# Prologue of an adaLN, gated scan and FP4 FFN block: modulation rows of both batches from one product, reordered setup

## The reference

```python
mod = (silu(c) @ wmod).reshape(2, 6, 1, 512)       # c: (2, 512), wmod: (512, 3072)
sa, ca, ga, sb, cb, gb = (mod[:, n] for n in range(6))
ga, gb = (sign(g) * max(abs(g), 0.25) for g in (ga, gb))
h = layernorm(x) * (1 + ca) + sa                    # x: (2, 4096, 512)
xn = h / max(norm(h), eps) * 512**0.5 * gamma
q, kv, a = split(xn @ W_qkva.T, 3)                  # W_qkva: (1536, 512)
y[t] = sigmoid(a[t]) * y[t-1] + kv[t]               # scan along the tokens
x = x + ga * (q * y)
h = layernorm(x) * (1 + cb) + sb
x = x + gb * ffn(h)     # silu(gate) * up, then down; every operand quantised in blocks of 16
```

## Time and profile before

| | us |
|---|---|
| runs | 1975.07, 1972.27, 1974.67 (median 1974.67) |
| the profiled execution | 1973.16 |
| its span | 1971.4 |
| TensorE busy | 1939.8 (98%) |
| VectorE busy | 1708.0 (87%) |
| GpSimd busy | 1200.2 (61%) |
| ScalarE busy | 631.6 (32%) |

### The profile page before, as it was taken

One profiled execution on the slowest core, in us unless ns is written; L12 is line 12 of the kernel. 1 busy time (PEld: TensorE's weight loads), 2 busy tenths in 40 slices (PEclk: granted clock), 3 DMA queues, 4 the chain that ended last, 5 costly groups with the idle time before them and its releaser, 6 DMA issues.

```text
span 1971.4 us, 27185 instructions
## 1 busy us (share of the span) xinstructions
PE 1939.8 (98%) x9403; PEld 928.5 (47%) x9403; DVE 1708.0 (87%) x2106; ACT 631.6 (32%) x885; POOL 1200.2 (61%) x1072
## 2 busy tenths in 40 slices
PE   8999999999999999999999999999999999999998
PEld 3444444444444444444444444444444444444443
DVE  7777687778778999999999999999999999999985
ACT  4333433343323333232323323323323232332321
POOL 1545556465635777677667767767766766776731
PEclk9999999999999999999999999999999999999999
DMA  8865665657552433433333343343343334334232
GB/s 291 278 164 161 161 168 151 171 154 179 130 125 74 91 90 72 93 87 72 86 93 72 79 98 75 75 96 83 72 90 89 72 83 96 72 78 100 69 73 65
DMA packets 421251, 218.22 MB, mean 111 GB/s; under 512 B 359858, under 2 KB 359870, under 8 KB 421188
## 3 DMA queue, kind: packets, MB, share of 16 engines
q1 hardware_dynamic: 421188, 217.39, 44.3%
HBM read 95.43 MB, written 33.57 MB: 65 GB/s over the span
## 4 chain that ended last, share of the span: by engine, by line
PE 82%; POOL 6%; DVE 6%; issue 2%; ACT 2%; DMA 2%; SPq 1%; DVEq 0%; ACTq 0%; POOLq 0%
PE bank L1050 43%; PE bank L969 15%; PE bank L1070 14%; PE bank L1074 7%; POOL arena L556 2%; POOL arena L558 2%; DMA arena<-arena 1%; SPq L396 1%; DVE arena L1145 1%; PE bank L994 1%; DVE bn L1134 1%; PE bank L908 1%; DVE arena L1274 1%; ACT arena L708 0%; ACT arena L725 0%
## 5 line engine op out<-in xcount | busy, mean ns | idle before, releaser
L1050 PE MATMUL bank<-wgu_hi,arena 128*128 128x512 f16 (+1 forms) x3072 | 869.3, 361 | 2.0 <-DVE arena L1383 2.0
L1050 PE MATMUL bank<-wgu_lo,arena 128*128 128x512 f16 (+1 forms) x1536 | 555.0, 361 | 0.0
L969 PE MATMUL bank<-arena,wq_hi 128*128 128x512 f16 x1536 | 458.8, 380 | 8.1 <-DMA arena<-arena 8.1
L1050 PEld LDWEIGHTS bank<-wgu_hi,arena 128*128 128x128 f16 x3072 | 300.6, 98 | 310.0 <-issue 2.4
L969 PE MATMUL bank<-arena,wq_lo 128*128 128x512 f16 x768 | 292.0, 380 | 0.0
L1070 PE MATMUL bank<-wd_hi,arena 128*128 128x512 f16 x693 | 262.7, 379 | 0.1
L1070 PE MATMUL bank<-wd_lo,arena 128*128 128x512 f16 x693 | 262.6, 379 | 0.0
L969 PEld LDWEIGHTS bank<-arena,wq_hi 128*128 128x128 f16 x1536 | 149.8, 98 | 185.7 <-DMA arena<-arena 11.5
L1050 PEld LDWEIGHTS bank<-wgu_lo,arena 128*128 128x128 f16 x1536 | 150.3, 98 | 153.7
L1383 DVE SCALAR_TENSOR_TENSOR arena<-bank,small,arena 128x512 f32<-128x512 f32 (+1 forms) x192 | 134.0, 700 | 87.4 <-PE bank L1050 81.5
L648 POOL TENSOR_TENSOR arena<-arena 128x512 f32<-128x512 f32 x63 | 153.1, 2431 | 92.5 <-DVE arena L1458 92.5
(11 more groups left out here) (162 smaller groups left out, 2778.1 us busy)
## 6 DMA issues: line engine op xcount, KB each, us to landing
arena<-in_L_attn_x_dram SPq DMA_DIRECT2D x32, 1024.0 KB, 5.6
arena<-x_scratch SPq DMA_DIRECT2D x128, 256.0 KB, 3.2
x_scratch<-arena SPq DMA_DIRECT2D x16, 1024.0 KB, 4.3
out_dram<-arena SPq DMA_DIRECT2D x64, 256.0 KB, 3.1
arena<-in_L_wmod_dram SPq DMA_DIRECT2D x6, 1024.0 KB, 14.4
arena<-arena SPq DMA_TRANSPOSE x258, 3.5
wgu_hi<-in_L_ffn_w_gate_dram SPq DMA_DIRECT2D x1, 2816.0 KB, 12.4
wgu_lo<-in_L_ffn_w_up_dram SPq DMA_DIRECT2D x1, 2816.0 KB, 19.0
```

What stands on the lines that cost most here:

```text
L969: last = pe.matmul(dst[m % 2][:, :].rearrange("p (j t) -> p j t", j=NJ), w[:, k, at], uT[p][:, half, :, k, :], start=(n == 0), stop=(n == ...
L1050: last = pe.matmul(dst[n][:, 0:w], xT[p][:, half, k, :], wt[:, k, cut], start=(m == 0), stop=(m == 3 * KD - 1))
```

## The change

- `silu_wide` holds for each k 64 columns of batch 0 and 64 of batch 1: one product gives the row of batch 0 on partitions 0 to 63 and that of batch 1 on 64 to 127. Two products (ca, sa) take the place of four, and each row is copied in two halves of 64 partitions, to both halves of its target. ScalarE copies 1 + ca of both batches (four copies ahead of `apply(0, 0)`) and sa of batch 1 (two), VectorE sa of batch 0 (two).
- Twelve transposes of the identity into a bank not yet used stand on TensorE ahead of the first mix product.
- wmod part 0 comes in two DMAs, and `mix_row(1)` waits for each half.
- Scale-and-shift of group 0: GpSimd makes tiles 0 and 1, VectorE tiles 2 and 3.
- `ffn_row(0)` stands between weight tiles 3 and 4, `ffn_row(1)` behind the maxima; ScalarE copies both (`copy_early_row`). `ffn_row(2)` stays in group 0. VectorE loses `copy_row(0)` and `copy_row(1)`.
- ga's product moves behind product_a(0, 0, 0), weight tile 8 behind it, and `turn_ga` behind product_kv(0, 0, 0).
- SyncE: wmod parts 4 and 3 are loaded between the parts of W_qkva, x of group 1 only after the transposes of group 0.

```diff
@@ banks and rows
-        MIX_ROWS = ((1, 0, one_ca, 1.0, bank[0]), (0, 0, sa, 0.0, bank[1]), (1, 1, one_ca, 1.0, bank[3]),
-                    (0, 1, sa, 0.0, bank[2]))
+        WQ_BANKS = [bank[n] for n in (5, 6, 7, 4, 1, 5, 6, 7, 1, 0, 5, 6)]
+        WQ_AFTER = (0, 0, 0, 0, 0, 1, 2, 3, 5, 0, 6, 7)
+        MIX_ROWS = ((1, bank[2]), (0, bank[3]))
+        EARLY_ROWS = 2
+        EARLY_BANK = (bank[0], bank[2])
@@ sync
-                load_modulation(0)
+                for k in range(0, KD, 2):
+                    sp.dma_start(wmod_part(0)[:, k:k + 2], w_mod_part[0][:, k:k + 2]).then_inc(part0_loaded[k // 2], 16)
...
+                load_qkva(2)
+                load_modulation(ROWS[0][0])
+                load_qkva(1)
+                load_qkva(0)
+                load_modulation(ROWS[1][0])
                 load_modulation(2)
-                sp.dma_start(xs[1], x_group[1]).then_inc(xs_loaded[1], 16)
...
+                sp.dma_start(xs[1], x_group[1]).then_inc(xs_loaded[1], 16)
                 load_maximum(raw_gate, w_gate, 0)
-                for part in (4, 3, 5):
-                    load_modulation(part)
+                load_modulation(ROWS[2][0])
@@ gpsimd, adaln
-                    for j in range(NJ if i else 0):
+                    if i == 0:
+                        pool.wait_ge(mix_row_copied, 4)
+                        pool.wait_ge(sa0_copied, 2)
+                    for j in range(NJ if i else POOL_J):
@@ scalar
-                copy_mix_row(0)
+                copy_mix_row(0, 0)
+                copy_mix_row(0, 1)
                 apply(0, 0)
-                copy_mix_row(1)
+                copy_mix_row(1, 1)
                 squares(0, 0)
-                copy_mix_row(2)
+                copy_early_row(0)
                 u_hi(0, 0)
-                copy_mix_row(3)
...
-                    if n == KD:
+                    if n == KD - 1:
+                        copy_early_row(1)
+                    if n == 2 * KD:
                         copy_ga_row()
@@ tensor
+                for n in range(12):
+                    pe.transpose(bank[7][:, 0:P], ident[:, :], ident[:, :]).then_inc(warm, 1)
                 pe.wait_ge(silu_wide_ready, 1)
                 pe.wait_ge(gamma_copied, 1)
                 mix_row(0)
                 mix_row(1)
                 for n in range(4):
                     turn_wq(n)
-                pe.wait_ge(mix_row_copied, 2)
-                for n in range(4, 6):
-                    turn_wq(n)
-                mix_row(2)
-                mix_row(3)
-                pe.wait_ge(mix_row_copied, 3)
+                ffn_row(0)
+                turn_wq(4)
+                pe.wait_ge(mix_row_copied, 6)
+                pe.wait_ge(sa0_copied, 2)
                 turn_maximum(bank[3], col("part_max", 4), max_ready, max_turned)
                 spread_maximum(bank[3], col("top_diagonal", 4)[0:4, :], max_diagonal, max_all)
-                pe.wait_ge(wmod_loaded[2], 16)
-                pe.wait_ge(mix_row_copied, 4)
...
-                for n in range(6, 9):
+                ffn_row(1)
+                for n in range(5, 8):
                     turn_wq(n)
@@ tensor, group 0
                         product_a(0, 0, 0)
-                        for n in range(9, NWQ):
+                        ga_product()
+                        for n in range(8, NWQ):
                             turn_wq(n)
-                        turn_ga()
+                        pe.wait_ge(ga_row_copied, 1)
                         pe.wait_ge(wq_split, 2 * KD)
                         product_kv(0, 0, 0)
+                        turn_ga()
...
-                        for n in range(NROW):
+                        for n in range(EARLY_ROWS, NROW):
                             ffn_row(n)
@@ vector
+                dve.wait_ge(mix_row_ready, 2)
+                for half in range(2):
+                    dve.tensor_copy(sa[half * HP:(half + 1) * HP, 0, :], bank[3][0:HP, :]).then_inc(sa0_copied, 1)
                 part_maximum(0, 2)
-                dve.wait_ge(mix_row_copied, 2)
-                for j in range(NJ):
+                dve.wait_ge(mix_row_copied, 4)
+                dve.wait_ge(sa0_copied, 2)
+                for n, j in enumerate(range(POOL_J, NJ)):
...
@@ vector, group 0
                         mix(0, 0, 0, 1, True)
-                        copy_row(0)
-                        copy_row(1)
                         u_lo(1, 1)
                         copy_row(2)
```

More of the change, by code:

```diff
@@ L199, in adaln_block_kernel @@
         wmax_turned, wmax_diagonal = sem("wmax_turned"), sem("wmax_diagonal")
-        wmod_loaded = [sem(f"wmod_loaded{n}") for n in range(6)]
+        wmod_loaded, part0_loaded = [sem(f"wmod_loaded{n}") for n in range(6)], [sem(f"part0_loaded{n}") for n in range(2)]
         ident_zero, ident_ready = sem("ident_zero"), sem("ident_ready")
@@ L894, in mix_row @@
                 def mix_row(n):
-                    part, b, _, _, space = MIX_ROWS[n]
-                    pe.wait_ge(wmod_loaded[part], 16)
+                    part, space = MIX_ROWS[n]
+                    if part:
+                        pe.wait_ge(wmod_loaded[part], 16)
                     for k in range(KD):
-                        last = pe.matmul(space[:, :], silu_wide[:, b, k, :], wmod_part(part)[:, k, :],
+                        if part == 0 and k % 2 == 0:
+                            pe.wait_ge(part0_loaded[k // 2], 16)
+                        last = pe.matmul(space[:, :], silu_wide[:, k].rearrange("p b m -> p (b m)"), wmod_part(part)[:, k, :],
                                          start=(k == 0), stop=(k == KD - 1))
@@ L903, in ffn_row @@
                 def ffn_row(n):
+                    space, ready = (EARLY_BANK[n], early_row_ready) if n < EARLY_ROWS else (t_bank[0], mod_ready)
                     pe.wait_ge(wmod_loaded[ROWS[n][0]], 16)
-                    wait(pe, mod_copied, n - 1)
                     for k in range(KD):
-                        last = pe.matmul(ROW_BANK[n][0:B, :], silu_c[:, k, :], wmod_part(ROWS[n][0])[:, k, :],
+                        last = pe.matmul(space[0:B, :], silu_c[:, k, :], wmod_part(ROWS[n][0])[:, k, :],
                                          start=(k == 0), stop=(k == KD - 1))
-                    last.then_inc(mod_ready, 1)
+                    last.then_inc(ready, 1)
                 def turn_wq(n):
@@ L937, in _, with ga_product @@
                     turn_wq(n)
-                pe.wait_ge(mix_row_copied, 2)
-                for n in range(4, 6):
-                    turn_wq(n)
-                mix_row(2)
-                mix_row(3)
-                pe.wait_ge(mix_row_copied, 3)
+                ffn_row(0)
+                turn_wq(4)
+                pe.wait_ge(mix_row_copied, 6)
+                pe.wait_ge(sa0_copied, 2)
                 turn_maximum(bank[3], col("part_max", 4), max_ready, max_turned)
                 spread_maximum(bank[3], col("top_diagonal", 4)[0:4, :], max_diagonal, max_all)
-                pe.wait_ge(wmod_loaded[2], 16)
-                pe.wait_ge(mix_row_copied, 4)
-                for k in range(KD):
-                    last = pe.matmul(bank[2][0:B, :], silu_c[:, k, :], wmod_part(2)[:, k, :],
-                                     start=(k == 0), stop=(k == KD - 1))
-                last.then_inc(ga_row_ready, 1)
-                for n in range(6, 9):
-                    turn_wq(n)
+                ffn_row(1)
+                for n in range(5, 8):
+                    turn_wq(n)
+                def ga_product():
+                    pe.wait_ge(wmod_loaded[2], 16)
+                    pe.wait_ge(early_row_copied, EARLY_ROWS)
+                    for k in range(KD):
+                        last = pe.matmul(bank[2][0:B, :], silu_c[:, k, :], wmod_part(2)[:, k, :],
+                                         start=(k == 0), stop=(k == KD - 1))
+                    last.then_inc(ga_row_ready, 1)
                 def turn_ga():
@@ L1182, in part_maximum @@
                                       apply_absolute_value=True).then_inc(max_ready, 1)
+                dve.wait_ge(mix_row_ready, 2)
+                for half in range(2):
+                    dve.tensor_copy(sa[half * HP:(half + 1) * HP, 0, :], bank[3][0:HP, :]).then_inc(sa0_copied, 1)
                 part_maximum(0, 2)
[L1185 to L1186 removed]
+                dve.wait_ge(mix_row_copied, 4)
+                dve.wait_ge(sa0_copied, 2)
+                for n, j in enumerate(range(POOL_J, NJ)):
                     dve.wait_ge(xhat_ready, j + 1)
                     dve.tensor_tensor(u[:, j, :], u[:, j, :], one_ca[:, 0, :], ALU.mult).then_inc(ca0_ready, 1)
[L1189 removed]
+                    dve.wait_ge(ca0_ready, n + 1)
                     dve.tensor_tensor(u[:, j, :], u[:, j, :], sa[:, 0, :], ALU.add).then_inc(h0_ready, 1)
```

59 lines of the change are left out of this document (36 added, 23 removed).

## The result

| | before | after |
|---|---|---|
| median of 11 runs (us) | 1974.19 (1972.27 to 1976.54) | 1979.81 (1976.85 to 1983.14) |
| ratio, 95% interval | | 1.0027 [1.0019, 1.0035] |
| the profiled execution, its span | 1973.16, 1971.4 | 1983.14, 1980.2 |

5.6 us slower; 1979.3 was forecast. The profiled execution of after is the slowest of its eleven, 10.0 us above that of before; its rows show the mechanism, and the medians show its size. I read the rows in the order of the prediction.

The account below looks back on a forecast made before the run. The prediction took the adaLN chain through VectorE, not TensorE, to bound the kernel. A ga copy 5.8 us late less 0.25 of slack gave +5.55 us on a mean of 1973.8: 1979.3, range 1974.0 to 1983.5.

Parts of the forecast that it names:

- the sum: Whole kernel: D of 5.8 less 0.25 of slack makes group 4 and the kernel 5.55 us later.
- What bounds the kernel: From the prologue to group 4: the adaLN chain through VectorE decides, not TensorE's products; slack at most 0.3 us.
- The ga copy: VectorE, group 0: the turn of ga ends at S + 10.8 = 47.7, so the copy comes 5.8 us later than 41.87.
- S: Start of product_a(0) on TensorE, group 0: 36.9 instead of 35.94, bounds 35.0 and 39.
- case (a): Rival, prologue: transposes don't raise the clock; second product ends at 16.6, S = 38.9, D = 7.8, +7.5: 1981.3; chance 0.25.
- the lift: Prologue, TensorE: twelve transposes bring full clock to the first mix products, gain between 0 and 2.6 us; second ends at 14.4.
- The new wait: TensorE before group 1's first product: about 6 us waiting for mix(0,2), which VectorE ends at 83.2.
- D: Delay of the ga copy on VectorE, +5.8 us, said to reach the start of group 4 whole.
- TensorE cannot win it back: Behind group 4: the +5.55 us stays, as TensorE's later waits follow the same chain.

Follow-up runs that it names:

- experiment 1: Changed kernel with VectorE taking the statistics of group 1 between weight splits 7 and 8, ahead of the ga copy: 1972.7 us, ratio 0.9993.
- experiment 2: Kernel before with only turn_ga moved, from before product_kv(0,0,0) to behind product_a(0,0,1): 1979.63 us, ratio 1.0028.
- experiment 4: Changed kernel with 28 small matmuls behind weight tile 4, in TensorE's idle time before the maxima: 1977.36 us, ratio 1.0013.
- experiment 3: Changed kernel, two runs: without the twelve transposes 1979.35 us, ratio 1.0026; with ten matmuls in their place 1980.97 us, ratio 1.003.
- experiment 5: Changed kernel with 26 small matmuls ahead of group 1's first product, in TensorE's wait for mix(0,2): 1975.5 us, ratio 1.0006.
- experiments 7 and 8: Changed kernel with experiment 4's matmuls and group 1's statistics earlier; 7 also reorders group 1's load, scaling, squares: 1970.88 us; 8 has no such reordering: 1970.4 us.

## Why the prediction was right

The mechanism held, and so did the sum, but only because terms were off in opposite directions.

- **What bounds the kernel.** Shown by experiments 1 and 2: moving only ga's turn costs 4.9 us, freeing only the statistics takes off 7.1. The rival that TensorE's own later order costs the time falls with experiment 1, which leaves that order as it is.
- **The ga copy.** The copy was forecast at S + 10.8; it comes at S + 11.25 (49.74 - 38.49), as the turn only starts 10.8 us behind S, where the sum had it end. The copy came 7.87 us later, by case (a) 7.8; in experiment 1, where full rate followed the transposes, it came at 47.55 (forecast 47.7).
- **The start of group 0, S.** 36.9 with the lift, 38.9 without. Measured 36.30 (experiment 1) and 38.49. The reason given was partly wrong. I had u_lo(0) and the transposes 1.05 later and deciding; in experiment 1 the first u_lo stands at 27.55, not late at all (27.57 in the earlier trace rows). In the profiled execution after it is 2.1 later, but what ended last was the second FFN row at half clock: I took half of its records to be slow, as in the earlier trace rows; after idle stretches of 6.0 to 7.7 us it takes 5.33 to 6.20. The chain of u was close behind: with the row at 3.60 (experiment 4) the transposes let product_a(0) start at 38.06, so the slow row decided by 0.4 us only.
- **The lift by the transposes.** My forecast took it, the profiled execution did not have it, and in the median neither leaving the transposes out nor matmuls in their place can be told from the changed kernel (experiment 3). The profiled execution is case (a), which had a chance of 0.25; what the median execution does is not known. The Trainium skill (TensorE: Matmul & The Clock Gate, Part 4: PE-mode transpose) has it that transposes don't count as busy for the full clock; the profiled execution after agrees (six of the records behind them took 5.24 us), the one of experiment 1 does not (eight took 3.67 behind them, after 1.06 us of idle time).
- **The new wait.** Forecast about 6 us, ended at 83 (by the same sum 85 in case (a)); measured 5.81, ended at 85.15.
- **The term that was missing.** I let group 4 be late by D less 0.25: 5.55, or 7.55 without the lift. It was 8.42: the means of group 2 come 7.45 late, those of group 3 8.5 (125.86, against 117.39 before). Between them lies group 1 at half clock, the price of the wait itself. Experiment 5 takes this away: the means of group 3 are then 7.0 late, group 4 comes 1.6 us earlier, and the median falls by 4.3. In experiment 2, whose wait there is 2.76, group 1's records have the length of full clock. The Trainium skill (TensorE: Matmul & The Clock Gate, HAM oscillation) warns of this: waits for data make TensorE start the next work at half clock. The runs agree for this wait, with the numbers above.
- **"TensorE cannot win it back".** This step does not hold as it stands. Against the profile of before, the delay shrinks from 8.42 at group 4 to 7.55 at the first FFN product after the change, and from 7.93 to 3.75 in the kernel without the transposes, whose profiled execution (1979.63) is nearer to the median of after (1979.81). In the median of experiment 2, too, 6.1 us at group 4 cost 4.9.
- **Why the sum came out.** The median, 5.6 over before, lies between the forecast's 5.1 over this median and case (a) with 7.1. Three things were off: the sum counted on the lift, which the profiled execution lacked (D 7.87 instead of 5.8); it had nothing for group 1 at half clock (up to 4.3 in the median); and it let none of the delay be absorbed behind group 4. That these cancelled was luck; that the sign and the place were right was not. The profiled pair, 10.0 us apart, does not give the 5.6 us of the medians, and no trace of an execution of after near its median was taken.

## What to carry to other kernels

Before moving an instruction, look at what stands behind its consumer in another engine's stream: here a copy of 0.15 us was the gate of the next group's statistics, and moving the statistics ahead of it took off 7.1 us, where the 7 us of mix products removed in front of a wait went into the wait (1.7 us before, 7.5 after). And price a new wait of TensorE twice, its length and the stretch at half clock that may follow; where the wait can't be removed, matmuls without a purpose in it paid 2.5 and 4.3 us in the median. Take several traces before you place a gain of a few us in a long kernel: here one stretch that no edit touched takes 437 us in some and 441 in others. A change that removes work from an engine at a place where it waits anyway gives it only a longer wait, and here a colder clock.

## What the runs showed of the hardware that I had not expected

- A dozen f32 transposes of 128 x 128 (2.82 us) were followed by products at full rate in one profiled execution (experiment 1, eight records in 3.67) and began at half rate in the six others that have them (after: six records in 5.24; all sixteen take 9.30 to 9.76 us), with the same instructions before them. With ten matmuls in their place the sixteen took 7.33, with neither 8.69, one execution each.
- TensorE's granted clock fell to 0.50 in or behind the idle stretches of 5.8 to 7.7 us each time, eleven in seven traces. The 28 matmuls of experiment 4 kept it at 1.00 in that execution, but with the same 28 in experiments 7 and 8 it fell around 32 us, behind the short waits at the maxima (1.25 and 0.74 us). Around waits of 2 to 3 us it is open: not behind the 2.76 us of experiment 2 or the 3.12 us wait of experiment 1 that ends at 195.4, but in the kernel before around its 3.0 us wait that ends at 196.4 and its 2.15 us wait that ends at 553.6. Two stretches of that kernel:

```profile
196.00:200.00 4.00, 3.56 (x13) 2.40 (x14) 2.36 (x4) 1.84 (x4) 3.84 (x4) 0.57 0.68 167
552.00:558.00 6.00, 4.36 (x13) 1.66 (x14) 0.68 (x1) 0.10 (x1) 0.00 (x0) 0.73 0.78 152
```

- The places of such falls differ between the profiles of nearly equal kernels. The mean granted clock of an execution goes with its time: for the kernel before, run beside the experiments, 28 executions at 0.997 have a mean of 1973.7 us, 16 at 0.995 have 1975.3 and four at 0.993 have 1977.6; for the changed kernel it goes from 1982.1 (two at 0.992) to 1977.1 (two at 0.995). So part of the scatter goes together with the clock; which of the two is the cause no run here shows.
- Keeping group 1 from half clock is worth more in the median than in the groups next to it: 4.3 us against 1.6 up to group 4. The rest was not attributed.
- f32 scale-and-shift on GpSimd (1.28) beside VectorE's takes 1.59 to 1.72, VectorE's 0.69 takes 1.08 to 1.74. Both slow down, and neither of the two splits that were run was better.
